# The pass for the softmax maxima in 64x64 tiles, with stationaries fetched dense and widened on chip

## The reference, cut to what matters

```
q, k, v = (xn @ W.T + b).reshape(16, 256, 16, 8)
p       = (pos_emb @ Wpos.T).reshape(511, 16, 8)
content = einsum('bthd,bshd->bhts', q + u_bias, k)
pos     = rel_shift(einsum('bthd,phd->bhtp', q + v_bias, p))
attn    = softmax((content + pos) / sqrt(8), axis=-1)
ctx     = einsum('bhts,bshd->bthd', attn, v) @ Wout.T + bout
```

## Time and profile before

| | us |
|---|---|
| three runs | 1078.78, 1071.94, 1071.25 (median 1071.94) |
| profiled execution | 1072.0 |
| its span, first to last instruction | 1070.1 |
| PE busy | 850.5 (79%) |
| DVE busy | 723.9 (68%) |
| ACT busy | 460.0 (43%) |
| POOL busy | 397.1 (37%) |

### The profile page before, as it was taken

The page is one execution under the profiler, slowest core; times in us unless marked ns, Lnnn a source line. Parts: engine busy times, 40 slices in busy tenths (PEclk is TensorE's granted clock), DMA queues, the critical chain, the costliest instruction groups (busy, mean ns, idle before and its releaser), DMA issues.

```text
span 1070.1 us, 21831 instructions
## 1 busy us (share of the span) xinstructions
PE 850.5 (79%) x8587; PEld 644.0 (60%) x8587; DVE 723.9 (68%) x1573; ACT 460.0 (43%) x773; POOL 397.1 (37%) x446
## 2 busy tenths in 40 slices
PE   2483679999999999987457998999999697057774
PEld 1243468888888888875434655666666377025553
DVE  6772435565555655533577888878788588989994
ACT  3860023333333333334455555656556554222331
POOL 6463001433334334335333334434243207323544
PEclk7696789999999999999669999999999899578998
DMA  6056111333243333453100000000000000000111
GB/s 140 1 159 216 42 39 38 79 75 65 67 94 72 72 65 69 90 153 74 25 1 1 2 2 2 2 2 2 1 2 1 1 1 1 0 0 2 23 26 32
DMA packets 69743, 46.45 MB, mean 43 GB/s; under 512 B 35184, under 2 KB 60984, under 8 KB 68920
## 3 DMA queue, kind: packets, MB, share of 16 engines
q1 hardware_dynamic: 52776, 24.72, 10.2%
q0 software_dynamic: 8032, 19.11, 7.0%
q10 hardware_dynamic: 8832, 1.22, 0.7%
HBM read 30.05 MB, written 12.06 MB: 39 GB/s over the span
## 4 chain that ended last, share of the span: by engine, by line
PE 40%; DVE 27%; DMA 9%; POOL 6%; SPq 6%; ACT 6%; issue 5%; ACTq 0%; POOLq 0%; DVEq 0%
PE PS L1059 7%; PE PS L1174 5%; PE PS L1175 5%; PE PS L1176 5%; PE PS L1079 4%; PE PS L1039 3%; PE PS L1063 3%; PE PS L1040 3%; DMA REG<-inverse_sums 3%; SPq L349 2%; DVE HB L1797 2%; DVE XX L1457 2%; DVE REG L1592 2%; DVE XX L1463 2%; DVE AM L1448 2%
## 5 line engine op out<-in xcount | busy, mean ns | idle before, releaser
L1573 DVE TENSOR_REDUCE MX<-PS 128x2 f32<-128x512 f32 x256 | 171.5, 686 | 165.4 <-PE PS L1040 163.7
L776 ACT ACTIVATE REG<-PS 128x1024 f32<-128x1024 f32 x128 | 131.5, 1027 | 242.1 <-PE PS L1063 239.4
L1059 PE MATMUL PS<-XX,TB 96*128 96x64 f16 x2048 | 160.2, 246 | 7.7 <-DMA XX<-NEG 4.5
L1039 PE MATMUL PS<-TM,YY 128*128 128x256 f16 x512 | 129.6, 285 | 31.7 <-DMA YY<-REG 14.9
L1059 PEld LDWEIGHTS PS<-XX,TB 96*128 96x128 f16 x2048 | 133.6, 120 | 23.2 <-issue 12.8
L613 POOL TENSOR_TENSOR HH<-HB,HH 128x512 f16<-128x512 f32 x64 | 75.8, 1184 | 173.8 <-ACT HH L833 173.8
L1040 PE MATMUL PS<-KM,YY 128*128 128x256 f16 x512 | 126.7, 279 | 0.0
L863 ACT ACTIVATE SG<-PS 128x512 f32<-128x512 f32 x128 | 76.2, 595 | 112.1 <-PE PS L1176 111.8
L1797 DVE SCALAR_TENSOR_TENSOR HB<-PS,SG 128x512 f32<-128x512 f32 x128 | 87.6, 684 | 46.0 <-ACT SG L863 46.0
L1063 PE MATMUL PS<-XX,KC 97*128 97x128 f16 x1024 | 108.0, 229 | 0.0
L1174 PE MATMUL PS<-XH,XX 128*128 128x512 f16 x256 | 98.8, 386 | 10.3 <-DVE HB L1797 10.1
(11 more groups left out here) (235 smaller groups left out, 1653.1 us busy)
## 6 DMA issues: line engine op xcount, KB each, us to landing
REG<-inverse_sums POOLq DMA_DIRECT2D x60, 128.0 KB, 3.1
YY<-queries_content ACTq DMA_DIRECT2D x224, 4.0 KB
KC<-keys_strips SPq DMA_DIRECT2D x16, 192.0 KB
keys_strips<-REG POOLq DMA_DIRECT2D x12, 224.0 KB, 7.8
R<-in_L_attn_x SPq DMA_DIRECT2D x32, 64.0 KB, 2.9
queries_position<-REG POOLq DMA_DIRECT2D x2, 960.0 KB, 12.9
queries_content<-REG POOLq DMA_DIRECT2D x2, 960.0 KB, 16.9
XX<-queries_position SPq DMA_DIRECT2D x60, 32.0 KB
```

The costliest lines, as they stand in the source:

```text
L776: A(P[jt][:, 1024 * up:1024 * up + 1024].rearrange("p (k x) -> p k x", k=2), ST[u % 2], ACT.Exp).then_inc(exp_done, 1)
L1039: mm(o, yp[:, a], TM[p][:, 31 - a:31 - a + T], start=True, stop=False)
L1059: mm(o_pos[:, a], TB[p][0:96, y0:y0 + 128], xp[0:96, 8 * bank + a], start=(a == 0), stop=False, skip_group_check=True)
L1573: nc.vector.tensor_reduce(MX[h % 2][:, 2 * kk:2 * kk + 2], banks[4 + kk % 2].rearrange("p (a j) -> p a j", a=2), AX_X, ALU.max)\
```

## The change

- YP and YC are half as wide: a stationary is 64 columns by 64 rows. Batches 0 to 7 (rows 0 to 63) and 8 to 15 (rows 64 to 127) are row halves, r; a from 0 to 15 and 16 to 31 are column halves, c, that write partitions 0 to 63 and 64 to 127. TM is loaded twice, one copy a row half. Row half r writes bank + r.
- A head has 8 bursts g of 2 x (4 position + 4 content) matmuls of 256 columns. A burst fills two banks (4 and 5; in the pass of head 0, which runs alone, 6 and 7 by turns with them), and one reduction takes 1024 elements.
- bursts(h) says behind which step they stand: in head h, g = 2 to 7 of head h + 1 behind k = 0, 2, ..., 10, and g = 0, 1 of head h + 2 behind k = 12 and 14; in head 0 all 8 of head 1 and two of head 2. Context parts move to k = 3 and 11.
- The stationaries come dense, one DMA of 128 rows x 256 each (YPD, YCD), issued by SP. They are widened to blocks by a multiplication with a column of 0 and 1 per row (C_OWN in CON, OWN in fp16): 16 pieces of 256 elements by ACT behind the exponentials of u = 0 to 4, for heads 2 on; 8 pieces of 512 by DVE for each of heads 0 and 1.
- The columns of XC, NAT_QU and NQB have another order (batch within groups of four), so that XC's rows are contiguous; NQB is written by two activations. The maxima's row takes 4 DMAs a half instead of 1, and its second half is awaited at k = 4 instead of 2 (BANKS has another order).
- Rows of the first three heads go to DRAM ahead of the rest. YP, YC and TM are no longer zeroed by POOL.

The diff, cut to its core (the rest are view sizes, counts of semaphores and column orders that follow from it):

```diff
-        YP, YC = ([YY[:, (2 * i + j) * N:(2 * i + j + 1) * N] for j in range(2)] for i in range(2))
+        YP, YC = ([YY[:, (2 * i + j) * N // 2:(2 * i + j + 1) * N // 2] for j in range(2)] for i in range(2))
...
+        YPD, YCD = ([YY[:, 2 * N + T * (2 * i + j):2 * N + T * (2 * i + j + 1)] for j in range(2)] for i in range(2))
...
+
+        def batch_pair(chunk):
+
+            b = 8 * (chunk % 2) + chunk // 2
+            return slice(b, b + 5, 4)
+
+        def bursts(h):
+
+            if h == 0:
+                slots = [(k, 1, g) for g, k in enumerate((0, 1, 3, 4, 6, 7, 9, 10))]
+            else:
+                slots = [(2 * g - 4, h + 1, g) for g in range(2, 8)]
+            return [slot for slot in slots + [(12, h + 2, 0), (14, h + 2, 1)] if slot[1] < H]
+
+        def maximum_banks(h, g):
+
+            return 6 if h == 0 and g % 2 else 4
...
-                sp.dma_start(TM[p][0:64, 0:287], window).then_inc(y_in[p], 16)
+                for half in range(2):
+                    sp.dma_start(TM[p][64 * half:64 * half + 64, 0:287], window).then_inc(y_in[p], 16)
...
             sp.wait_ge(prep_done, 4)
             for k, part in enumerate((0, 0, 1)):
                 sp.dma_start(pos_d[:, k, :, 0:NPOS], PT[:, part, 0:NPOS]).then_inc(pos_out, 16)
             sp.wait_ge(pos_out, 48)
-            sp.wait_ge(zeroed, 14)
+            def maximum_stationaries(h):
+
+                sp.dma_start(YPD[h % 2], qvb_d[DH * h:DH * h + DH, :].rearrange("d (k x) -> k d x", x=T)).then_inc(y_dense[h % 2], 16)
+                sp.dma_start(YCD[h % 2], qu_d[h, 0].rearrange("d (n t) -> n d t", n=B)).then_inc(y_dense[h % 2], 16)
+
+            first = slice(0, FIRST * DH)
...
             for h in range(2):
                 for k, part in enumerate((0, 0, 1)):
                     sp.dma_start(k4_d[h, :, k].rearrange("w d x -> d w x"),
                                  NAT[NAT_K + part][DH * h:DH * h + DH, :].rearrange("p (w x) -> p w x", w=4)).then_inc(k_first, 16)
-            sp.wait_ge(khi_first, 16)
-            for h in range(2):
-                maximum_keys(h)
-            sp.wait_ge(high_done, 16)
-            maximum_queries(0, NQB[0:DH, :])
+            sp.wait_ge(qvb_first, 16)
+            sp.wait_ge(qu_first, 16)
+            maximum_stationaries(0)
             sp.wait_ge(stage, 16)
             first_position_queries(0)
             sp.wait_ge(k_first, 16 * 6)
             key_operands(0)
-            sp.wait_ge(stage, 24)
-            first_content_queries(0)
+            maximum_keys(1)
+            maximum_stationaries(1)
             key_operands(1)
-            maximum_queries(1, NQB[DH:2 * DH, :])
...
+                if h + 2 < H:
+                    sp.wait_ge(max_mm, 8 * h + 8)
+                    maximum_positions(h + 2)
+                    maximum_keys(h + 2)
+                    maximum_stationaries(h + 2)
                 if h + 1 < H:
-                    sp.wait_ge(max_mm, 16 * h)
-                    maximum_positions(h + 1)
-                    maximum_keys(h + 1)
-                    maximum_queries(h + 1, qvb_d[DH * h + DH:DH * h + 2 * DH, :])
                     sp.wait_ge(st_mm, 8 * h)
...
-                      bank.rearrange("p (b i) -> p b i", b=B), ACT.Identity, bias=VEC3[:, 1:2])
+                    for r in range(2):
+                        A(NQB[:, 2048 * r + 256 * (7 - chunk):2048 * r + 256 * (8 - chunk)].rearrange("p (w c i) -> p w c i", w=2, c=4),
+                          bank.rearrange("p (c w i) -> p w c i", c=4, w=4)[:, 2 * r:2 * r + 2], ACT.Identity, bias=VEC3[:, 1:2])
                 A(*natural(c, 0), ACT.Identity, bias=VEC3[:, kind:kind + 1]).then_inc(high_done, 1)
...
             def shift_row(n, half):
                 act.wait_ge(neg_ready, 2 * n + half + 1)
-                row = XC[n % 2][96:97, :].rearrange("p (m t a) -> p t m a", t=2, a=16)
-                act.dma_start(row[:, half], NEG[half][:, :]).then_inc(neg_in[half], 16)
...
+                row = XC[n % 2][96:97, :].rearrange("p (r m c t a) -> p r c t m a", r=2, m=64, c=2, t=2)
+                for r in range(2):
+                    for c in range(2):
+                        act.dma_start(row[:, r, c, half], NEG[half][64 * c:64 * c + 64, 8 * r:8 * r + 8]).then_inc(neg_in[half], 16)
...
+            def first_content_queries(h):
+
+                p, rows = h % 2, slice(DH * h, DH * h + DH)
+                for w in range(4):
+                    for k, part in enumerate(PARTS):
+                        to = 24 * w + 8 * k
+                        act.dma_start(XC[p][to:to + 8, 1024 * w:1024 * w + 1024],
+                                      NAT[NAT_QU + part][rows, 1024 * w:1024 * w + 1024]).then_inc(x_in[p], 16)
+
+            def widened(h, pieces):
+
+                p = h % 2
+                for piece in pieces:
+                    j = piece % 8
+                    if piece == 0:
+                        act.wait_ge(y_dense[p], Y_DENSE * (h // 2 + 1))
+                        act.wait_ge(max_mm, 8 * (h - 1))
+                    if piece < 8:
+                        to, queries = YP[p][:, :].rearrange("p (n s a) -> p s n a", n=8, s=8)[:, j], \
+                            YPD[p].rearrange("p (n a) -> p n a", n=8)
+                    else:
+                        to, queries = YC[p][:, T * j:T * j + T], YCD[p]
+                    last = A(to, queries, ACT.Copy, scale=CON[:, C_OWN + 8 - 8 * (piece // 8) + j:C_OWN + 9 - 8 * (piece // 8) + j])
+                    if piece % 2:
+                        last.then_inc(y_wide[p], 1)
+
             act.wait_ge(high_done, 24)
-            for h in range(2):
-                content_rows(h, NAT[NAT_QU][DH * h:DH * h + DH, :], range(B))
+            act.dma_start(qu_d[0:FIRST, 0], NAT[NAT_QU][0:FIRST * DH, :]).then_inc(qu_first, 16)
+            act.wait_ge(zeroed, 8)
+            act.wait_ge(stage, 24)
+            first_content_queries(0)
             shift_row(0, 0)
...
-                    if u in (4, 6) and h + 1 < H:
-                        shift_row(h + 1, (u - 4) // 2)
-                    if h + 2 < H:
-                        if u == 0:
-                            act.wait_ge(max_mm, 16 * h + 16)
-                        if h and u < 4:
-                            content_rows(h + 2, qu_d[h + 2, 0], range(4 * u, 4 * u + 4))
-                        elif not h and u >= 6:
-                            act.wait_ge(qu_out, 32)
-                            content_rows(h + 2, qu_d[h + 2, 0], range(8 * u - 48, 8 * u - 40))
+                    if u < 5 and h + 2 < H:
+                        widened(h + 2, range((0, 4, 7, 10, 13)[u], (4, 7, 10, 13, 16)[u]))
+                    if u in (3, 6) and h + 1 < H:
+                        shift_row(h + 1, (u - 3) // 3)
...
             pe.wait_ge(v_done, 8)
-            def maximum_scores(h, kk):
-
-                p, n = h % 2, 16 * h + kk
-                if kk == 0:
+            def maximum_scores(h, g):
+
+
+                p, n, bank = h % 2, 8 * h + g, maximum_banks(h, g)
+                if g == 0:
                     pe.wait_ge(y_in[p], Y_LOADS * (h // 2 + 1))
-                if n >= 2:
-                    pe.wait_ge(max_done, n - 1)
+                    pe.wait_ge(y_wide[p], 8 * (h // 2 + 1))
+                if h:
+                    pe.wait_ge(max_done, n)
+                elif g >= 2:
+                    pe.wait_ge(max_done, g - 1)
                 yp = YP[p][:, :].rearrange("p (m a) -> p a m", a=32)
                 yc = YC[p][:, :].rearrange("p (m a) -> p a m", a=32)
-                for half in range(2):
-                    a = 2 * kk + half
-                    o = banks[4 + kk % 2][:, T * half:T * half + T]
-                    mm(o, yp[:, a], TM[p][:, 31 - a:31 - a + T], start=True, stop=False)
-                    last = mm(o, yc[:, a], KM[p][:, :], start=False, stop=True)
+                for i in range(2):
+                    tiles = [(slice(64 * r, 64 * r + 64), 16 * c + 2 * g + i, banks[bank + r][64 * c:64 * c + 64, T * i:T * i + T])
+                             for r in range(2) for c in range(2)]
+                    for rows, a, o in tiles:
+                        mm(o, yp[rows, a], TM[p][rows, 31 - a:31 - a + T], start=True, stop=False)
+                    for rows, a, o in tiles:
+                        last = mm(o, yc[rows, a], KM[p][rows, :], start=False, stop=True)
                 last.then_inc(max_mm, 1)
...
-            for kk in range(16):
-                maximum_scores(0, kk)
+            for g in range(8):
+                maximum_scores(0, g)
             for h in range(H):
                 for k in range(16):
                     scores(h, k)
-                    if h + 1 < H and k < 12:
-                        for kk in range(16 * k // 12, 16 * (k + 1) // 12):
-                            maximum_scores(h + 1, kk)
-                    if h and k == 4:
+                    for follows, head, g in bursts(h):
+                        if follows == k:
```

(64 more changed lines are left out.)

108 lines of the change are left out of this document (52 added, 56 removed).

## The result

The changed kernel took 1046.48 us (median of 4 runs, 1040.03 to 1047.88), the one before 1073.32 (4 runs): ratio 0.974, 95% interval 0.969 to 0.979. Faster, as forecast, and inside the range, but 20 us above the forecast of 1026 and outside its own case (1018 to 1032, chance 0.45). The profiled execution took 1040.03 us (span 1038.1), so 14 of the 20 us can be read from its trace.

What follows compares the result with a forecast made beforehand. TensorE (PE) alone was taken to set the pace in the heads. Span 1070.1 less 16 (start), 25.4 (heads 1 to 13) and 4.9 (heads 14 and 15) gave 1023.8; forecast 1026 us, range 1004 to 1052.

Steps and rivals of the forecast that it cites:

- its own case: Whole kernel: the forecast's main case, a time of 1018 to 1032 us, chance 0.45.
- Four tiles side by side: Maxima bursts on PE: four 64x64 tiles run concurrently, so 16 matmuls take 4 rounds of 0.109, 0.44 us instead of 0.87.
- rivals 1 and 4: Bursts: 1, paced by weight loads or half overlapped, 1074 to 1081, chance 0.12; 4, tiles not concurrent, 1178, chance 0.05.
- B = 0.63: Time of one burst on PE in us: 0.44 for its rounds plus 0.19 for changing the tiling twice.
- The steady head: One head of attention in the loop: 20.35 us, a gain of 1.95 each, 25.4 over heads 1 to 13.
- ACT costs nothing: ACT's widening copies in the heads: 0.42 us each, 6.6 a head, ACT's 17 to 20 us fitting within 20.35.
- POOL's chain fits: POOL's chain for the sums in each head: takes 19.0 us and still fits in 20.35.
- The start, 16 us: Ahead of the heads: dense rows land earlier, so head 1 starts in effect at 143.5 against 159.5, gaining 16 us.
- rival 3: The start gains nothing, dense rows still later and DVE's order holding the reductions: 1041 us, chance 0.08.
- Heads 14 and 15: Last two heads: 3.3 us from head 14's six bursts, 1.6 from a shorter wait before head 15, together 4.9.
- Nothing changes behind the heads: Everything after the last context part was to stay unchanged, 572.8 us from 497.3.
- B = 0.82: A slower burst, in us, given as one of two ways to reach the range's high end of 1052.

Runs made afterwards that it cites:

- e2: Changed kernel with ACT's widening copies, from head 2 on, cut to one column each: 1045.18 us in one run.
- e12: e5 with POOL's five large copies to DRAM held until head 0's dense rows have landed, SP's order left as in the changed kernel: 1041.6 us.
- e6: Changed kernel with SP issuing heads 0 and 1's dense rows before head 0's position DMAs, and POOL's five large copies behind head 0's dense rows: 1031.9 us.
- e7: e6 with POOL's twelve copies of keys also held, until the first rows of two query copies have landed in DRAM: 1029.5 us.
- e5: Changed kernel with the bursts from head 1 on behind odd score chunks 1, 3, ... 15 instead of even ones: 1042.1 us.
- e10: e9 with DVE widening head 1's rows behind all of head 0's reductions, instead of a piece behind each: 1034.4 us.
- e9: e5 and e6 combined, but POOL's five large copies wait for all score operands of head 0, not just its dense rows: 1040.1 us.

## Why the prediction held, and where it was off

**What bounds the kernel**: right. PE is busy 20.75 of 20.75 us a head, and only its stream counts.

**Four tiles side by side**: right; rivals 1 and 4 are out. Four loads of 64 columns fit into each round of 0.11 us; they start within 0.01 us of each other and are all done 0.20 us later (the row of PEld above), so loads of different tiles overlap. The prediction weighed the Trainium skill, "TensorEngine Tiling (Array Packing)", Restrictions, with the Trainium skill, "TensorE: Matmul & The Clock Gate", LDWEIGHTS, against it, for a burst of 1.04 us if loads can't overlap. The trace doesn't agree with that case. It agrees with the Trainium skill, "TensorEngine Tiling (Array Packing)", Key Properties: "Different tiles can execute LdWeights and Matmul in parallel".

**B = 0.63** was mis-sized: 0.75. I had priced the change of tiling from the context part, as 0.09 in and 0.10 out. Those two were right, but the first round takes twice as long as the rest (0.22 against 0.11), and in a burst of four rounds that shows. Eight a head: +1.0 us. The Trainium skill, "TensorEngine Tiling (Array Packing)", Key Properties, says that a change of tiling drains the array; the runs put 0.29 us on a burst's changes.

**The steady head** is 20.75, not 20.35 and above the 20 to 20.5 that were to show it, so 1.55 us are won and not 1.95. The bursts' 1.0 is partly made up: no burst waited on a reduction in the steady heads (I had 0.3), and a score step takes 0.68 us (433.23 to 433.91 above), not 0.70, another 0.3. Over 13 heads: 20.2 us instead of 25.4.

**ACT costs nothing**: right. The waits for exponentials on PE's side from 181 to 430 us:

```profile
PEld PS L1102 <- ACT REG L819: 4.9, 12, 0.4
```

They are waits of weight loads, 0.4 us in each of 12 heads, under a matmul stream that is busy without a gap; e2 shows that they cost nothing.

**POOL's chain fits**: right, with little left. It waited for the context 3.1 us in 12 heads where it had been 121.4 in 13. That it now ends later against PE shows behind the heads (below).

**The start, 16 us**: this step failed; it brought 3.5. Counted back from the third context part (170.6 less 12 score steps of 0.68, six bursts of 0.75 and a context part of 1.9), head 1 starts at 156.0 in effect, not at 143.5. I wrote that SP reaches the two dense DMAs at 81.5 "as before" and that they land by 90. It reached them at 93, since the six copies to keys_strips now stand behind a wait and took 17.2 us to issue, where the kernel before had

```profile
67.10 9.34 SPq L398 DMA_DIRECT2D keys_strips<-REG  x6
```

and the rows were there at 110.4. The term that the sum goes by is the next one, head 1's rows, issued behind all this: 107.5 in the prediction, 118.55 in the trace, 11.05 us late, and step k = 4 of head 0 is 11.2 late (138.7 for 127.5). From there to head 1 it took 17.3 us instead of 16.0; in this my sum had a slip (12 steps, eight bursts and a context part are 15.4, not 14.7), and the rest is B.

The prediction had seen that SP's issues were slow while POOL's copies were under way, and took this as a price of an issue. But the DMA engines were full there, in the kernel before too (share 1.01 from 79 to 95 us), and that delays landings as well: DVE had head 0's rows 10.5 us after SP had issued them, in e12, with POOL's five copies held back, 1.6 us after. SP itself was no earlier for that (92.5 in e12, 92.3 in e6); with the copies of the keys held back too it reached the dense rows at 84.7 (e7). No single one of these is the 12.5 us: e6, with order and gate, brings 159.3 in place of 170.6 in the third context part, 11.3 of them; e12, with the gate alone, 2.0 against e5, since head 1's rows stay at 117.6. The condition of rival 3 ("dense rows still later") was the true one, and its chance of 0.08 too low.

**Heads 14 and 15** brought more than 4.9: 31.9 us in all until the last context part, less 20.2 and 3.5, leaves 8.2. The wait for the row ahead of head 15 is 1.45 us (it was 4.49, I had 2.9), which explains 1.5 of the 3.3. The other thing that I had left out is the clock behind that wait; first the kernel before, then the changed one:

```profile
477.30:484.00 6.70, 6.27 (x60) 4.93 (x64) 0.00 (x0) 1.02 (x1) 1.04 (x1) 0.50 1.06 270
```
```profile
452.10:458.90 6.80, 6.78 (x120) 6.18 (x124) 0.00 (x0) 4.10 (x4) 1.70 (x1) 1.00 0.85 180
```

In the kernel before, three score steps and a context part took 6.97 us there (477.73 to 484.70); by their pace at granted clock 1.00 they take 4.0. So 3.0 us more are saved, less a new wait of 0.9 us for an exponential at 447.3. The forecast had no term for either; that they bring it closer to the measured time is luck.

Together, for the profiled execution: 12.5 + 5.2 - 3.3 = 14.4 us above the forecast span of 1023.8, against 14.3 measured (1038.1). As the 8.2 of heads 14 and 15 is what was left over, this sum has to close and proves nothing by itself.

**Nothing changes behind the heads** (574.8): so it was in this execution, with 574.7, but by luck. DVE's multiplication of the last head's context waits for POOL's chain; in the kernel before, the changed one and e10:

```profile
508.80 1.22 DVE L1631 TENSOR_TENSOR REG<-REG 128x1024 f32<-128x1024 f32 x1 [2.78 <-DMA REG<-inverse_sums]
```
```profile
478.79 1.23 DVE L1701 TENSOR_TENSOR REG<-REG 128x1024 f32<-128x1024 f32 x1 [1.70 <-DMA REG<-inverse_sums]
```
```profile
473.40 1.23 DVE L1703 TENSOR_TENSOR REG<-REG 128x1024 f32<-128x1024 f32 x1 [3.77 <-DMA REG<-inverse_sums]
```

From the last context part that is 13.5, 15.4 and 21.0 us (14.5 to 19.0 in the others of the table): the change made this wait 1.9 us longer. Why e10's is the longest I haven't followed. What comes behind it, the same instructions in all kernels, took 561.3 us before and 559.3 after, so that the 1.9 us were made up. In the other profiles it took 559.0 to 564.4; where they part, a stretch at granted clock 0.50 falls on other work (e9 above). The median lies 6.4 us above the profiled execution; which part of the kernel that is in stays open, as the other runs have no profile.

**The range.** The high end holds a slip: B = 0.82 alone gives 1045 to 1049 by the prediction's own formula, not 1052. That the result lies inside the range is owed to its width: the start had failed nearly as in rival 3 (1041), and B was mis-sized besides.
